# A Mamba scan kernel with a feed-forward tail: GpSimd forms the dbx products of two state columns in one operation, from a ring of six columns, and the B rows are asked for in another order

## The reference

```python
xz = x_in @ W_in
x, z = (xz[..., :D], xz[..., D:])
proj = x @ W_x
B_ssm = proj[..., D:D + N]
C_ssm = proj[..., D + N:]
delta = softplus(proj[..., :D] @ W_dt + b_dt)
dA = exp(einsum('bld,dn->bldn', delta, A))
dBx = einsum('bld,bln->bldn', delta * x, B_ssm)
# per token t:  h = dA_t * h + dBx_t ;  y_t = einsum('bdn,bn->bd', h, C_t)
y = (y + x * D_param) * silu(z) @ W_out        # then residual and layernorm
...
out = r * (square(relu(xk @ W_k.T)) @ W_v.T)   # feed-forward, r = sigmoid(xr @ W_r.T)
```

## Time and profile before

| what | value |
|---|---|
| time, median of 3 runs | 942.09 us (941.38 to 942.38) |
| the profiled execution: its own time | 944.42 us |
| its span, first to last instruction | 942.6 us |
| granted TensorE clock, mean over the span | 0.973 of full speed |
| busy share of the span: PE, DVE, ACT, POOL | 92%, 96%, 90%, 94% |
| b products, c products on GpSimd (128x1024) | 255, 122 |

### The profile page before, as it was taken

The page is one execution under the profiler, slowest core; times in us unless marked ns, Lnnn a source line. Parts: engine busy times, 40 slices in busy tenths (PEclk is TensorE's granted clock), DMA queues, the critical chain, the costliest instruction groups (busy, mean ns, idle before and its releaser), DMA issues.

```text
span 942.6 us, 15838 instructions
## 1 busy us (share of the span) xinstructions
PE 864.2 (92%) x5024; PEld 688.7 (73%) x5024; DVE 900.9 (96%) x985; ACT 847.9 (90%) x2064; POOL 889.1 (94%) x399
## 2 busy tenths in 40 slices
PE   8757679999999899989999899998999999999998
PEld 5545567877878587787868678786778768778876
DVE  4899989999999999999999999999999999999896
ACT  5886988989999999998999999999999999978875
POOL 4999999999999999999999989999999999999970
PEclk9987898999999999999999999999999999999999
DMA  7445435462534644455463644446354354446231
GB/s 222 156 177 204 175 138 204 179 235 104 210 157 161 239 164 172 183 178 166 174 248 147 224 148 160 179 179 248 125 210 179 143 198 179 157 160 223 91 101 45
DMA packets 49938, 163.60 MB, mean 174 GB/s; under 512 B 5248, under 2 KB 33152, under 8 KB 33600
## 3 DMA queue, kind: packets, MB, share of 16 engines
q1 hardware_dynamic: 48528, 161.27, 46.2%
q0 software_dynamic: 512, 1.31, 0.5%
q10 hardware_dynamic: 816, 0.02, 0.1%
HBM read 153.15 MB, written 9.44 MB: 172 GB/s over the span
## 4 chain that ended last, share of the span: by engine, by line
PE 46%; ACT 28%; DVE 15%; issue 9%; DMA 1%; POOL 0%; POOLq 0%; DVEq 0%; SPq 0%; ACTq 0%
PE w_ps L1326 10%; ACT da_ps L654 10%; PE y_ps L1317 9%; PE w_ps L1350 6%; DVE da_ps L1033 5%; PE w_ps L1359 4%; PE w_ps L1362 4%; DVE hg L1049 3%; DVE hg L1033 3%; PE w_ps L1465 3%; DVE hg L1040 2%; PE w_ps L1368 2%; ACT xn_tok L591 2%; ACT h_tok L591 2%; ACT zs L715 2%
## 5 line engine op out<-in xcount | busy, mean ns | idle before, releaser
L542 POOL TENSOR_TENSOR dbx<-u,b_ring 128x1024 f32<-128x1024 f32 x255 | 599.4, 2380 | 4.7 <-DVE hg L1033 4.6
L654 ACT ACTIVATE da_ps<-delta,a_neg 128x512 f32<-128x512 f32 x512 | 340.0, 684 | 23.9 <-DVE hg L1040 7.3
L555 POOL TENSOR_TENSOR hg<-hg,c_ring 128x1024 f32<-128x1024 f32 x122 | 290.4, 2381 | 8.5 <-ACT carry L660 6.7
L1317 PE MATMUL y_ps<-ident,hg 128*128 128x128 f32 x2048 | 264.3, 279 | 9.2 <-POOL hg L555 9.0
L1317 PEld LDWEIGHTS y_ps<-ident,hg 128*128 128x128 f32 x2048 | 241.7, 145 | 35.9 <-issue 17.8
L1033 DVE TENSOR_TENSOR_SCAN da_ps<-da_ps,carry,dbx 128x512 f32<-128x512 f32 x203 | 249.8, 1271 | 4.3 <-ACT da_ps L654 4.1
L1033 DVE TENSOR_TENSOR_SCAN hg<-da_ps,carry,dbx 128x512 f32<-128x512 f32 x181 | 220.3, 1263 | 1.4 <-ACT carry L660 1.2
L1040 DVE TENSOR_TENSOR hg<-da_ps,c_ring 128x1024 f32<-128x1024 f32 x68 | 82.3, 1210 | 0.2
L1049 DVE TENSOR_TENSOR hg<-da_ps,c_ring 128x512 f32<-128x512 f32 x130 | 82.3, 673 | 0.0
L1033 DVE TENSOR_TENSOR_SCAN da_ps<-da_ps,dbx 128x512 f32<-128x512 f32 x64 | 75.8, 1213 | 3.3 <-ACT da_ps L654 2.8
L1326 PE MATMUL w_ps<-xnT_ring,w_in 128*128 128x512 f32 x120 | 61.4, 636 | 16.0 <-ACT xT L696 14.1
(11 more groups left out here) (212 smaller groups left out, 1333.0 us busy)
## 6 DMA issues: line engine op xcount, KB each, us to landing
c_ring<-bc_rows_dram SPq DMA_DIRECT2D x64, 1024.0 KB, 4.7
b_ring<-bc_rows_dram SPq DMA_DIRECT2D x63, 1024.0 KB, 6.7
xres<-in_L_attn_x_in_dram SPq DMA_DIRECT2D x16, 512.0 KB, 4.8
x_tok<-in_L_attn_x_in_dram SPq DMA_DIRECT2D x15, 512.0 KB, 5.9
out_dram<-r_out SPq DMA_DIRECT2D x14, 512.0 KB, 3.2
bc_rows_dram<-bc_rows SPq DMA_DIRECT2D x64, 16.0 KB, 5.4
w_in<-in_L_attn_W_in_dram SPq DMA_DIRECT2D x2, 256.0 KB, 4.3
x_tok<-in_L_attn_x_in_dram SPq DMA_DIRECT2D x2, 256.0 KB, 4.6
```

Source lines behind the costliest of these rows:

```text
L542: pool.tensor_tensor(dbx[:, n % X_RING, :, :], u[:, ip, :, :], b.to_broadcast([P, KH, LC]), ALU.mult).then_inc(s["dbx_done"], 1)
L555: pool.tensor_tensor(part, part, c_of(n).to_broadcast([P, KH, LC]), ALU.mult).then_inc(s["g_pool"], 1)
L654: act.activation(da_of(n, h), delta[:, ip, h, :], ACT.Exp, scale=a_neg[:, h, n:n + 1]).then_inc(s["da_ready"], 1)
L1317: last = pe.matmul(y_tok[:, b, h * P:(h + 1) * P], hg[:, n % H_RING, h, b * P:(b + 1) * P], ident[:, :], is_transpose=True, start=n == 0 a ...
```

## The change

GpSimd makes the b products of two neighbouring columns in one operation, 128x2048 elements, with u repeated for both columns and each B row repeated for both halves (the new function times_b_twice). The pairs are (0,1), (2,3), ... and stand at the even places, four places ahead: at place n the pair (n + 4, n + 5). The ring has six columns instead of four, and a pair starts once column n - 1 is scanned, as a single product at place n did. Only columns 0 and 1 of the first chunk are still made one by one. The c products are unchanged (C_RUN = 1 keeps them single) and keep their places. Of SP's order, load_b(t, 2) is moved ahead of load_c(t, 1) and of the load of x_tok, load_b(t, 3) ahead of load_c(t, 2), load_b(t + 1, 0) ahead of load_c(t, 3), and load_b(t + 1, 1) ahead of load_c(t + 1, 0).

```diff
-X_RING = 4
+X_RING = 6
+C_RUN = 1
-B_LEAD, C_LAG, Y_LAG = 3, 1, 2
+B_LEAD, C_LAG, Y_LAG = 4, 1, 2
...
+        def dbx_of(i, n):
+            return (NS * i + n) % X_RING
...
                 if scan:
+                    load_b(t, 2)
                     if not (t == 0):
                         load_c(t, 1)
                 if more:
                     need(sp, s["xn_done"], t + 2)
                     sp.dma_start(x_tok[:, :, :], x_v[t + 2]).then_inc(s["x_loaded"], 16)
                 if scan:
-                    load_b(t, 2)
+                    load_b(t, 3)
                     load_c(t, 2)
-                    load_b(t, 3)
...
-                if scan:
-                    load_c(t, 3)
                 if pre:
                     need(sp, s["bc_stored"], 16 * TB * (t + 2))
...
                     load_b(t + 1, 0, start)
+                if scan:
+                    load_c(t, 3)
+                if pre:
+                    if not start:
+                        load_b(t + 1, 1)
                     load_c(t + 1, 0, start)
-                    load_b(t + 1, 1, start)
                     if start:
+                        load_b(0, 1, True)
                         load_c(0, 1, True)
...
+            def times_b_twice(i, ip, n):
+
+                need(pool, b_loaded[n // GN], 16 * (i + 1))
+                for m in range(KH):
+                    need(pool, s[f"u{m}_done"], i + 1)
+                need(pool, s["scan_done"], KH * (NS * i + n + 1 - X_RING + 1))
+                at, row = dbx_of(i, n), n % GN
+                b = b_ring[:, n // GN % BG, row:row + 2, :]
+                pool.tensor_tensor(dbx[:, at:at + 2, :, :], u[:, ip, :, :].unsqueeze(1).to_broadcast([P, 2, KH, LC]),
+                                   b.unsqueeze(2).to_broadcast([P, 2, KH, LC]), ALU.mult).then_inc(s["dbx_done"], 2)
...
                 for n in range(NS):
                     ahead = column_at(t, par, n + B_LEAD, scan, pre, mid)
-                    if ahead:
+                    if ahead and ahead[0] == 0 and ahead[2] < HEAD_COLS:
                         times_b(*ahead)
+                    elif ahead and ahead[2] % 2 == 0:
+                        times_b_twice(*ahead)
```

More of the change, by code:

```diff
@@ L362, in column_at, with c_of, products_of @@
             return (t, par, n) if scan else None
-        def c_of(n):
-            return c_ring[:, n // GN % BG, n % GN:n % GN + 1, :]
+        def c_of(n, k=1):
+            return c_ring[:, n // GN % BG, n % GN:n % GN + k, :]
+        def dbx_of(i, n):
+            return (NS * i + n) % X_RING
+        def products_of(i):
+            runs = []
+            for n in whole_of(i):
+                if i == LAST and n == NS - 1:
+                    break
+                if runs and len(runs[-1]) < C_RUN and runs[-1][-1] == n - 1 and n % GN:
+                    runs[-1].append(n)
+                else:
+                    runs.append([n])
+            return runs
         def da_of(n, h):
@@ L541, in times_b, with times_c @@
                     return
-                pool.tensor_tensor(dbx[:, n % X_RING, :, :], u[:, ip, :, :], b.to_broadcast([P, KH, LC]),
+                pool.tensor_tensor(dbx[:, dbx_of(i, n), :, :], u[:, ip, :, :], b.to_broadcast([P, KH, LC]),
                                    ALU.mult).then_inc(s["dbx_done"], 1)
-            def times_c(i, n):
+            def times_b_twice(i, ip, n):
[7 more added lines that the diff above has]
+                                   b.unsqueeze(2).to_broadcast([P, 2, KH, LC]), ALU.mult).then_inc(s["dbx_done"], 2)
+            def times_c(i, run):
+                n, k = run[0], len(run)
                 need(pool, c_loaded[n // GN], 16 * (i + 1))
@@ L550, in times_c @@
                 if ends(i):
-                    need(pool, s["scan_done"], KH * (NS * i + n + 1))
+                    need(pool, s["scan_done"], KH * (NS * i + run[-1] + 1))
                 else:
-                    need(pool, s["carry_saved"], kept_wholes(i, n))
-                part = hg[:, n % H_RING, :, :]
-                pool.tensor_tensor(part, part, c_of(n).to_broadcast([P, KH, LC]), ALU.mult).then_inc(s["g_pool"], 1)
+                    need(pool, s["carry_saved"], kept_wholes(i, run[-1]))
+                slot = n % H_RING
+                part = hg[:, slot:slot + k, :, :]
+                pool.tensor_tensor(part, part, c_of(n, k).unsqueeze(2).to_broadcast([P, k, KH, LC]),
+                                   ALU.mult).then_inc(s["g_pool"], k)
             def step(t, par, pre=False, scan=False, mid=False, end=False, late=False, more=False):
@@ L560, in step @@
                     ahead = column_at(t, par, n + B_LEAD, scan, pre, mid)
-                    if ahead:
+                    if ahead and ahead[0] == 0 and ahead[2] < HEAD_COLS:
                         times_b(*ahead)
+                    elif ahead and ahead[2] % 2 == 0:
+                        times_b_twice(*ahead)
                     behind = column_at(t, par, n - C_LAG, scan, pre, mid)
[L564 to L569, removed]
+                    for run in products_of(behind[0]) if behind else []:
+                        if behind[2] == run[-1]:
+                            times_c(behind[0], run)
             def close():
@@ L1032, in scans @@
                     out = da_of(n, h) if in_bank else hg[:, n % H_RING, h, :]
-                    dve.tensor_tensor_scan(out, da_of(n, h), dbx[:, n % X_RING, h, :],
+                    dve.tensor_tensor_scan(out, da_of(n, h), dbx[:, dbx_of(t, n), h, :],
                                            0.0 if first else carry[:, n, h:h + 1], ALU.mult, ALU.add).then_inc(s["scan_done"], 1)
```

## The result

The changed kernel is slower by 0.3%, of about the size and at the place that the forecast named.

The account below looks back on a forecast made before the run. VectorE was taken as the bound, 99% busy at 55.5 us per step, with GpSimd behind only in the first chunk. Start +2.3 us, middle 0 and end 0 took the median from 942.09 to 944.4 us; range 941.2 to 947.5.

Parts of the forecast that it names:

- The pair: GpSimd's paired b product: 4.49 us to the next start against 4.62 for two singles, record 4.61; bounds 4.07 to 4.62.
- The middle and the end: Steps after the start and the last chunk: 0 us each; VectorE's 55.5 us step unchanged, GpSimd's saving becomes idle time.
- The loads: SP's moved loads in the middle: they change nothing, keeping pace with the earlier use of the B rows.
- The start: First chunk, where GpSimd never waits: c products 13 and 15 come 3.4 and 3.2 us late, costing 2.3 us.
- second chain: Start: late c product 15 delays TensorE's B and C matmuls; could give 3.2 us, taken to run beside the 2.3.
- TensorE's wait: Sign in the first chunk: TensorE waits near 6.5 us for column 13's c product, where it was 5.03.
- VectorE and dbx: Sign against the forecast: it is wrong if VectorE waits for dbx anywhere.
- The thin cover of the C rows: Start: C rows of columns 12 to 15 land at 68.25, needed at 68.36; a stall up to 2.3 us adds nothing.
- Absorbed delay: Rival in the start: pair costs 4.25 or less, or TensorE's add_ups run at full speed; 942 to 943 us, chance 0.28.
- bound GpSimd: Rival: a pair dearer than 4.77 us makes GpSimd set the step; 958 us at 4.9, chance 0.09.
- late c product in the middle: Rival: the 2.4 us cover goes and TensorE's matmuls slip in every step; 946 to 949 us, chance 0.08.
- gain in the middle: Rival: VectorE's idle time there shrinks because GpSimd is always early; about 6 us, 936 us, chance 0.06.

Follow-up runs that it names:

- after_old_loads: The changed kernel with SP's loads put back in the order of the kernel before: 967.36 us, ratio 1.0254 to the kernel before.
- before_loads: The kernel before with only the changed order of SP's loads, nothing else: 944.45 us, ratio 1.0015 to the kernel before.
- after_again: The changed kernel once more, unchanged, for a second profile: 945.38 us in a single execution.
- start_single: The changed kernel with single b products, in the places of before, through column 3 of chunk 1, pairs after: 943.53 us, ratio 1.0012 to the kernel before.
- c_first: The changed kernel with the c product queued ahead of the pair at each place: 943.26 us, ratio 1.0008 to the kernel before.
- two_singles: The changed kernel with each pair made as two single products in the same place: 947.33 us, ratio 1.0046 to the kernel before.
- before_again: The kernel before once more, unchanged, for its spread and a second profile: 942.47 us, ratio 0.9997.

## Why the prediction was right

**The bound** was right: VectorE at 55.5 us per step in both kernels. GpSimd is busy for 213.47 us of the 222 from 180 to 402, so it idles 2.1 us for each of the four steps, as named.

**The pair** was right: 4.48 us apart, 4.55 in the record, against 4.49 and 4.61. The Trainium skill, "GPSIMD Engine Reference", section 3.1, gives 4497 ns; the spacing here is 17 ns less and the record 53 ns more, so the page's figure was closer to the spacing, and the 1.0 us that I drew from comparing it with the record did not come.

**The middle and the end** were right: 222.0 us for four steps in both (262.59 to 484.57 before, 263.45 to 485.44 after), and 46.3 us from the gate of step 15 to that of the last step in both profiles. The walk through the queue held as well: the pair (2,3) starts at 351.85, c product 13 at 356.35 and c product 15 at 363.18, each 0.9 us after the forecast place, which is what the whole changed profile lags behind the first one of before at that point. The loads were right only for this kernel: they keep pace with the pairs and no stall for rows stands in the first profile, but 22 us hang on them (after_old_loads) and beside single products they cost 0.9 us that a row shows (before_loads).

**The start** had the right place, and its size was 2.3 forecast and 3.0 measured between medians. c product 13 at 81.63 (81.6 forecast) and 15 at 88.44 (88.4) fit. Which chain would decide was half wrong. The transposes came 2.02 us late instead of 2.3, but ran at full clock, 1.04 us at a granted 1.00 instead of 1.94 at 0.50, and so delivered the exponential only 89.17 - 87.99 = 1.18 us late; VectorE's stall there was to be 2.9 and was 1.52. TensorE's B and C matmuls came 92.73 - 89.49 = 3.24 us late, as the text had worked out for its second chain (3.2), and this chain brought a second stall of 1.50 us. The second chain set the sum, where I had let it run beside the first.

The two stalls are 3.02 us together. Against the first profile of before, from which the forecast was worked out and which has 0.60 us of stall there, that is 2.42 more and looks like the 2.3; this closeness is luck, since the first chain gave 0.9 of it and the second 1.5. Against the second profile of before, whose own transposes already ran at full clock (1.07 us at 85.49) and which has no stall listed there, all of it is loss, and that is the difference between the medians. So the term was 0.7 us too small for two reasons: I took the smaller of its two values, and I worked it out from an execution that carried a part of the loss already.

**TensorE's wait** for column 13's c product was to be near 6.5 us and was 8.42. That sign did not follow from my own sum: 5.03 us and a product that comes 3.4 us later make 8.4. In the second profile of before this wait is 6.40.

**VectorE and dbx.** I was to be wrong if VectorE waited for dbx anywhere. The only such wait in the changed kernel's profiles is 0.30 us at 25.17, and it stands in before too, at 25.06.

**The thin cover of the C rows** was real: 0.79 us of stall at 69.13 in after_again, none in the first profile. Both reach the same gate time, so it does run beside the main term.

**The rivals.** Absorbed delay: neither of its conditions occurred (a pair costs 4.48, and the two add_ups take 3.49, near the half clock's 3.67); what did run at full clock were the transposes behind them, and they took 0.9 us out of the first chain only. No bound GpSimd, no late c product in the middle, no gain in the middle. start_single, c_first and two_singles show that the order in the start carries most of the loss: it follows the order and not the form of the operation, and 1.7 and 2.1 of the 3.1 us at the first gate go with it. The last 1.0 to 1.4 us in those two kernels stand beside waits of VectorE of another kind, for C rows and for a late pair; that nothing else is in it is argued from the rows, and which kernel reaches exactly the time of before cannot be told with intervals of 0.13% to 0.15%.

## What to carry to other kernels

A cheaper operation on an engine that has slack gained nothing by itself here; it made room, and the gain came only when work was moved from the bound engine into that room (here -8.9 us for the changed kernel, +5.8 for the kernel before by the same edit). When two operations become one, ask for every queue what now stands ahead of the small operation that another engine waits for, and look first at the part of the program where this engine never idles: there exchanging neighbours was worth 2 us. And a lead that grows by one column needs its loads to grow with it: without that this kernel was 2.5% slower than before.

## What the runs showed of the hardware

Executions of one kernel fall into groups some 2 us apart (before_again: nine from 941.3 to 942.8, three from 944.1 to 944.5), and the two profiles of before show where such 2 us come from: from when TensorE's granted clock comes back. Windows of TensorE in the first profile of before, then in the second (busy, count, granted clock, transfers' share, GB/s):

```profile
104.00:111.00 7.00, 0.84 (x8) 0.94 0.00 1
111.00:115.00 4.00, 3.91 (x6) 0.50 0.26 74
115.00:119.00 4.00, 4.00 (x22) 0.75 1.01 420
```

```profile
104.00:111.00 7.00, 0.76 (x6) 0.80 0.01 1
111.00:115.00 4.00, 4.00 (x8) 0.50 0.22 82
115.00:119.00 4.00, 4.00 (x26) 0.99 1.00 420
```

From 111 on both are at 0.50 of the clock, the 1.2 GHz level, after TensorE had idled 6.25 and 6.24 us. In the second the clock had fallen earlier in this pause (mean 0.80 instead of 0.94) and is back from 115 on (0.99 instead of 0.75). The same eight add_ups there, each kernel's timeline in turn:

```profile
114.66 1.91 PE L1317 MATMUL y_ps<-ident,hg 128*128 128x128 f32 x8
```

```profile
114.32 1.40 PE L1317 MATMUL y_ps<-ident,hg 128*128 128x128 f32 x8
```

In the first profile the transposes and output matmuls behind them are late with them, ScalarE's copies and its exponential follow, and VectorE stalls 1.83 us at 121 us, where it stalls 1.03 at 120 in the second; a like stall of 1.13 us at 148 us is missing from the second. The profiles of c_first, two_singles and before_loads have the same two stalls, 1.77 to 1.96 us and 1.13; in these four the second gate comes 57.5 to 57.6 us after the first, and in before_again, start_single and both profiles of the changed kernel 55.6 or 55.7. The profile of before_loads, at 947.04, shows a third place: the eight set-up matmuls at 6.91 us took 3.76 us, where the other profiles have 1.99, and all that follows is 2 us late. So in a start that TensorE's chain sets, one execution can differ from the next by as much as this change is worth, and one profile against one profile (944.42 and 945.26) would have told 0.8 us where the medians tell 3.0. What makes the clock fall and come back earlier in one execution than in another is open; I had no run for it.

The other surprise: two operands that are each read with a stride of 0, u over the two columns and the B rows over the two halves, in an operation of 2048 elements, cost GpSimd nothing that shows. Two singles take 4.62 us, the pair 4.48; the 0.14 us saved are one operation's fixed part (0.13 by the half product).
